# A third bank for the sums: the bias written ahead by ScalarE, and weight pieces that pass through the transposes' banks

## The chip, the cores and the metric

The kernel runs on one core of a Trainium2 chip. The metric is the device time of one execution in microseconds (us); of the kernel before there are three runs, 358.68, 358.79 and 359.64, so the median is 358.79. The engines are named as in the profile: PE (TensorE; PEld its weight loads), DVE (VectorE), ACT (ScalarE), POOL (GpSimd) and SP (SyncE, which only issues DMAs here).

## The reference

The input x has 8 images of 1024 rows and 512 columns in f32. Of attention only the first 16 rows of an image reach the output (the array `iter_out` is zero beyond row E = 16), so the work is nearly all in the second half, which is done for all rows:

```
mod = (silu(c) @ wmod)                          # per image: sa, ca, ga, sb, cb, gb
h = layernorm(x) * (1 + ca) + sa
x = x + ga' * attention(h)                      # beyond row 16: x + ga' * bo
h = layernorm(x) * (1 + cb) + sb
xd, wd = h and weight, each block of 32 rounded to a grid of 6 bits and scaled back
x = x + gb' * (xd @ wd.T + bias)                # ga', gb': sign(g) * max(|g|, 0.25)
```

## The kernel before

There are 64 tiles of 128 rows, 4 to a group (16 groups), 8 to an image. One loop over q = 0 to 63 is written out by hand on each engine; "slot q" is what an engine does in that turn of the loop. All waits are on semaphores, and every engine works strictly in the written order.

For tile n the work is this. ACT sums and squares the rows (`sums`, `deviations`), DVE makes the scale (`scales`, L1198 to L1201), ACT normalises (`normalise`, L501), POOL multiplies and adds the modulation (L390, L397), DVE takes the block maxima, quantises and scales back (L1208, L1227, L1234; half of the last on POOL, L377). PE turns the tile with four transposes (`transposes`, L730) into one of two PSUM banks, 0 and 1. ACT copies the turned tile rounded to XH (`high_part`, L469), DVE subtracts XH and writes the remainder XL (`low_part`, L1184). PE then sums in one of two PSUM banks, 2 and 3 (`product`): eight matmuls from XH (L747, L748), four from XL (L752), and a thirteenth, L755, that adds gate times bias from the small matrix G. DVE adds the sum to x (`add_tile`, L1241), and SP stores a group.

The weights are scaled by the gate for each image and split as well into WH and WL, in four pieces. Images are counted from 0. For images 2 to 7, and for the unscaled weights that the first 16 rows need (counted as 8), the turned weights lie in SBUF; a piece costs ACT two instructions, the rounded copy WH (L479) and a copy to PSUM bank 4 (L481), and DVE one, WL (L1193). The table FOLDS gives the slots: image b's pieces are issued in slots 8b-4 to 8b-1, image 8's in slots 57 to 60. "Fold slots" below are these.

PE's order in slot q is: transposes of tile q+1, the product of tile q, then a piece of the attention work for the first rows (`head_work`). ACT's is: `high_part(q+1)`, a weight piece, attention work, normalising, deviations, sums. DVE's is: `add_tile(q-1)`, `low_part(q+1)`, a weight piece, the small scales, maxima, quantising, attention work. The attention work has three passes in slots 9 to 53 and a last part in slots 52 to 61 (AFTER = 51). `masks_row` (L1020) is a copy of a 2x640 array with conversion, which the attention needs at slot 15.

## Time and profile before

| what | value |
|---|---|
| median of three runs | 358.79 us |
| the profiled execution's own time | 358.5 us |
| its span (first to last instruction) | 356.7 us |
| PE busy | 320.0 us (90%) |
| DVE busy | 284.8 us (80%) |
| ACT busy | 239.4 us (67%) |
| POOL busy | 240.6 us (67%) |
| L755, the bias matmul | 64 of them, 25.2 us, 393 ns each |
| chain that ended last | PE 38%, DVE 25%, ACT 16%, POOL 9%, issue 9% |

A matmul's duration in the profile is longer than the step from one to the next, since matmuls overlap; what a matmul costs on a busy PE is the step between two starts. Idle time is given before the instruction that ended it, with what released it. The granted clock (PEclk) is 1.00 in most of the span.

### The profile page before, as it was taken

Reading aid. Unit: us, or ns where it says so; the run is one execution under the profiler, and the core shown is the slowest. Engines: PE = TensorE matmul, PEld = TensorE weight load, DVE = VectorE, ACT = ScalarE, POOL = GpSimd, SP = SyncE. Lnnn points to the kernel's source line nnn. Section 1 sums busy time; section 2 is a strip of 40 time slices with the busy share of each in tenths; the row PEclk is TensorE's granted clock in tenths of the full one; section 3 lists DMA queues with packets and bytes.
Section 4 is the critical chain, followed back from the end, with each engine's and each line's share of the span. In section 5 each row is a group of like instructions: output and inputs, shape, how many; then the busy total and the mean of one; then the engine's idle time right before and its main releaser. Section 6 shows DMA issues by size and latency. Waiting matters only on the chain.

```text
span 356.7 us, 6296 instructions
## 1 busy us (share of the span) xinstructions
PE 320.0 (90%) x2247; PEld 243.4 (68%) x2247; DVE 284.8 (80%) x498; ACT 239.4 (67%) x537; POOL 240.6 (67%) x142
## 2 busy tenths in 40 slices
PE   7997984958999989998999999979999989994994
PEld 5223653748998777786788778767887768673883
DVE  4899839947727997969898879797878989899832
ACT  3357463577968798789788899876779897231410
POOL 2339956059876896989599979984999499702000
PEclk9999998798999999999999999989999999999899
DMA  6999899972697097958698977597837962020122
GB/s 207 395 405 367 277 214 234 314 237 112 120 218 197 2 239 204 222 152 217 183 242 265 242 136 291 154 233 158 257 120 152 233 180 115 6 86 31 73 105 88
DMA packets 23797, 68.51 MB, mean 192 GB/s; under 512 B 2467, under 2 KB 2596, under 8 KB 19798
## 3 DMA queue, kind: packets, MB, share of 16 engines
q1 hardware_dynamic: 16224, 53.40, 43.8%
q0 software_dynamic: 7392, 14.68, 24.9%
q8 instruction: 18, 0.29, 0.3%
q14 instruction: 13, 0.11, 0.1%
q10 hardware_dynamic: 150, 0.02, 0.0%
HBM read 50.96 MB, written 17.14 MB: 191 GB/s over the span
## 4 chain that ended last, share of the span: by engine, by line
PE 38%; DVE 25%; ACT 16%; POOL 9%; issue 9%; DMA 1%; SPq 0%; DVEq 0%; POOLq 0%; ACTq 0%
PE ps L747 7%; PE ps L748 7%; PE ps L752 7%; ACT U L501 5%; PE ps L730 4%; ACT unused L514 3%; DVE XL L1184 3%; PE ps L832 3%; POOL U L390 3%; DVE DD L1234 2%; DVE Q L1227 2%; DVE amax L1208 2%; ACT XH L469 2%; DVE X L1241 2%; POOL U L397 2%
## 5 line engine op out<-in xcount | busy, mean ns | idle before, releaser
L747 PE MATMUL ps<-WH,XH 128*128 128x512 f32 x256 | 108.4, 424 | 6.0 <-DVE X L1241 4.2
L748 PE MATMUL ps<-WL,XH 128*128 128x512 f32 x256 | 102.4, 400 | 0.0
L390 POOL TENSOR_TENSOR U<-U,c_bc 128x1024 f32<-128x1024 f32 x31 | 76.4, 2466 | 19.7 <-ACT U L501 19.6
L397 POOL TENSOR_TENSOR U<-U,sb_bc 128x1024 f32<-128x1024 f32 x31 | 74.2, 2394 | 4.5 <-POOL U L390 0.2
L1184 DVE TENSOR_TENSOR XL<-ps,XH 128x512 fp32r<-128x512 f32 x64 | 43.9, 685 | 40.4 <-ACT XH L469 40.3
L752 PE MATMUL ps<-WH,XL 128*128 128x512 f32 x256 | 69.4, 393 | 1.5 <-DVE XL L1184 1.5
L469 ACT ACTIVATE XH<-ps 128x512 fp32r<-128x512 f32 x64 | 37.5, 586 | 47.5 <-PE ps L730 47.3
L501 ACT ACTIVATE U<-X,nmr,rstd 128x512 f32<-128x512 f32 x64 | 48.2, 807 | 28.6 <-DVE nmr L1201 26.0
L747 PEld LDWEIGHTS ps<-WH,XH 128*128 128x128 f32 x256 | 49.7, 194 | 17.1 <-DVE X L1241 5.4
L752 PEld LDWEIGHTS ps<-WH,XL 128*128 128x128 f32 x256 | 48.6, 190 | 12.7 <-DVE XL L1184 1.9
L748 PEld LDWEIGHTS ps<-WL,XH 128*128 128x128 f32 x256 | 49.8, 195 | 8.8
L1241 DVE TENSOR_TENSOR X<-ps,X 128x512 f32<-128x512 f32 x64 | 43.6, 681 | 5.1 <-PE ps L755 4.9
L525 ACT ACTIVATE unused<-X,negm 128x512 bf16<-128x512 f32 x64 | 45.6, 714 | 0.5
L730 PE MATMUL ps<-idf,DD 128*128 128x128 f32 x256 | 40.7, 284 | 5.3 <-DVE DD L1234 5.3
L514 ACT ACTIVATE unused<-X 128x512 bf16<-128x512 f32 x64 | 39.5, 619 | 5.6 <-POOL X L354 5.1
L1208 DVE TENSOR_REDUCE amax<-U 128x32 f32<-128x1024 f32 x32 | 38.7, 1210 | 4.4 <-POOL U L397 4.4
L730 PEld LDWEIGHTS ps<-idf,DD 128*128 128x128 f32 x256 | 31.9, 147 | 13.2 <-issue 8.4
L1227 DVE TENSOR_TENSOR Q<-U,ps 128x1024 fp8e4<-128x1024 f32 x32 | 39.0, 1218 | 0.2
L377 POOL TENSOR_TENSOR DD<-Q,s 128x1024 f32<-128x1024 fp8e4 x12 | 23.0, 1913 | 19.9 <-DVE Q L1227 19.9
L413 POOL TENSOR_TENSOR Wd<-Wb,gb_bc 128x512 f32<-128x512 f32 x24 | 30.3, 1293 | 3.8 <-issue 3.8
L1193 DVE TENSOR_TENSOR WL<-ps,WH 128x512 fp32r<-128x512 f32 x36 | 24.4, 685 | 3.4 <-ACT ps L481 3.2
L755 PE MATMUL ps<-G,pick 128*128 128x512 f32 x64 | 25.2, 393 | 0.0
(232 smaller groups left out, 443.8 us busy)
## 6 DMA issues: line engine op xcount, KB each, us to landing
X<-in_x SPq DMA_DIRECT2D x16, 1024.0 KB, 7.5
out<-X SPq DMA_DIRECT2D x15, 1024.0 KB, 6.0
X<-mod_scratch POOLq DMA_DIRECT2D x14, 1024.0 KB, 13.6
X<-in_wmod SPq DMA_DIRECT2D x2, 1024.0 KB, 12.2
sb_bc<-mod_scratch SPq DMA_DIRECT2D x7, 256.0 KB, 12.9
c_bc<-mod_scratch SPq DMA_DIRECT2D x7, 256.0 KB, 11.2
gb_bc<-mod_scratch SPq DMA_DIRECT2D x6, 256.0 KB, 5.7
X<-in_wmod SPq DMA_DIRECT2D x2, 512.0 KB, 4.7
```

The source lines that it names most:

```text
L390: nc.gpsimd.tensor_tensor(a, a, spread(c_bc[:, b % 2, :]), ALU.mult).then_inc(u_done, 2 if g == 0 else 1)
L397: nc.gpsimd.tensor_tensor(a, a, spread(sb_bc[:, b % 2, :]), ALU.add).then_inc(h_done, 2 if g == 0 else 1)
L501: A.activation(U[:, g % 2, j, :], X1[:, g % XSLOTS, j, :], ACT.Identity, bias=nmr[:, g % 2, j:j + 1], scale=rstd[:, g % 2, j:j + 1]).then_ ...
L514: A.activation(unused[:, j % 2, :], X1[:, g % XSLOTS, j, :], ACT.Identity, accum_out=total[:, j:j + 1]).then_inc(sum_done, 1)
L730: m = TR(ps[:, XT_BANK + n % 2, c * P:(c + 1) * P], DD[:, j, c * P:(c + 1) * P], idf[:])
L747: M(bank, XH[:, n % 2, r], WH[:, b % 2, k, :], start=k == 0, stop=False)
L748: M(bank, XH[:, n % 2, r], WL[:, b % 2, k, :], start=False, stop=False)
L752: M(bank, XL[:, n % 2, r], WH[:, b % 2, k, :], start=False, stop=False)
L1184: TT(XL[:, n % 2, :], ps[:, XT_BANK + n % 2, :], XH[:, n % 2, :].bitcast(F32), ALU.subtract).then_inc(xl_done, 1)
L1208: RED(amax[:, h, :], blocks(U[:, g % 2, HALF * h:HALF * (h + 1), :]), AX, ALU.max, apply_absolute_value=True).then_inc(am_done, 1)
L1227: TT(blocks(Q8[:, h]), blocks(U[:, g % 2, HALF * h:HALF * (h + 1), :]), wide(inv[:, h, :]), ALU.mult, saturate=False).then_inc(q_done, 1)
L1241: TT(a, ps[:, Y_BANK + n % 2, :], a, ALU.add).then_inc(o_done, 1)
```

## The change

From tile 16 on (WIDE) a sum rotates over three banks, 4, 2 and 3. ACT writes gate times bias, already spread over the 128 partitions, into the bank (`preset_bias`, in slot q for tile q+1, behind `high_part(q+1)` and the weight piece), and the product only adds to it: L755 goes for 48 tiles. The product waits for `preset` in place of the add of tile n-2; `preset_bias(n)` waits for the add of tile n-3. Six more DMAs on SP (256 KB each) bring the spread rows, into `v_bc` and a new tensor. Bank 4 is no longer free for the weights: from image 2 on a piece goes through bank 0 or 1, the one that tile q's transposes left, and the transposes of tile n wait for WL of the piece whose slot in FOLDS is n-3. One matmul (`open_third`) opens bank 4. `masks` now lies in a part of U until the first tile needs it, so `masks_row` runs at the start, ahead of `bias_rows`. Some semaphores are merged.

```
+WIDE = 16
+        bias_odd = sb("bias_odd", [P, D])
+        bias_bc = (v_bc[:], bias_odd[:])
+        mk = U[0:2, 0, 2:4, :].rearrange("p j d -> p (j d)")[:, 0:P + D]
+        def sum_bank(n):
+            return Y_BANK + n % 2 if n < WIDE else (W_BANK, Y_BANK, Y_BANK + 1)[(n - WIDE) % 3]
+        def piece_bank(q):
+            return XT_BANK + q % 2
@@ SP, in the loop over t
                     mod_row(gb_bc[:], b, GB, gb_in)
+                    if b == 2:
+                        sp.wait_ge(x1_done, 3)
+                    if b >= 4:
+                        sp.wait_ge(preset, 2 * TILES * (b - 1) - WIDE)
+                    mod_row(bias_bc[b % 2], b, GBIAS, bias_in[b % 2])
@@ ACT, weight_high
-                    act.wait_ge(wt_low, NC * b + k)
+                    act.wait_ge(xl_done, fold_slot(b, k) + 2)
                     A.copy(ps[:, bank, :], turned(b, k)).then_inc(w_copied, 1)
+            def preset_bias(n):
+                b = n // (2 * TILES)
+                act.wait_ge(bias_in[b % 2], 16 * (b // 2))
+                if n == WIDE:
+                    act.wait_ge(wt_mm, 3 * NC + 1)
+                else:
+                    act.wait_ge(o_done, n - 2)
+                A.copy(ps[:, sum_bank(n), :], bias_bc[b % 2]).then_inc(preset, 1)
             def normalise(g, h):
+                if g == 0 and h == 1:
+                    act.wait_ge(lrow_done, 1)
@@ ACT, slot q
-                    weight_high(*FOLDS[q - 1], W_BANK)
+                    b, k = FOLDS[q - 1]
+                    weight_high(b, k, W_BANK if b == 1 else piece_bank(q))
+                if WIDE <= q + 1 < LAST:
+                    preset_bias(q + 1)
@@ PE, transposes(n)
                     pe.wait_ge(xl_done, n - 1)
+                    if n - 3 in FOLDS and FOLDS[n - 3][0] > 1:
+                        b, k = FOLDS[n - 3]
+                        pe.wait_ge(wt_low, NC * b + k + 1)
@@ PE, product(n)
+                opens = n < WIDE
+                if not opens:
+                    pe.wait_ge(preset, n - WIDE + 1)
+                elif n >= 2:
                     pe.wait_ge(o_done, n - 1)
...
-                M(bank, pick[:, b:b + 1].to_broadcast([P, P]), G[:], start=False, stop=True).then_inc(y_done, 1)
+                if opens:
+                    m = M(bank, pick[:, b:b + 1].to_broadcast([P, P]), G[:], start=False, stop=True)
+                m.then_inc(y_done, 1)
+            def open_third():
+                pe.wait_ge(plain_cp, NC)
+                M(ps[:, W_BANK, :], onesr[:], G[:], start=True, stop=True).then_inc(wt_mm, 1)
+                if q == WIDE - 3:
+                    open_third()
@@ DVE
-                elif q == 1:
-                    masks_row()
...
             first_v()
+            masks_row()
             bias_rows()
-                    weight_low(*FOLDS[q - 1], W_BANK)
+                    b, k = FOLDS[q - 1]
+                    weight_low(b, k, W_BANK if b == 1 else piece_bank(q))
```

How this stands in ACT's order in slot 20 (a fold slot of image 3), up to slot 21's first row. XH is the turned tile, WH and the copy from Wd the weight piece, U the normalising. Before:

```order
L469 ACTIVATE XH<-ps 128x512 [waits xt_done,y_done]
L479 ACTIVATE WH<-Wd 128x512 [waits wscaled,y_done]
L481 COPY ps<-Wd 128x512 [waits wt_low]
L501 ACTIVATE U<-X,nmr,rstd 128x512 x2
L514 ACTIVATE unused,total<-X 128x512 [waits sum_done,x_added2]
L514 ACTIVATE unused,total<-X 128x512 [waits sum_done]
L469 ACTIVATE XH<-ps 128x512 [waits xt_done,y_done]
```

And now:

```order
L488 ACTIVATE XH<-ps 128x512 [waits xt_done,y_done]
L498 ACTIVATE WH<-Wd 128x512 [waits wscaled,y_done]
L501 COPY ps<-Wd 128x512 [waits xl_done]
L514 COPY ps<-v_bc 128x512 [waits o_done,bias_in0]
L534 ACTIVATE U<-X,nmr,rstd 128x512 x2
L547 ACTIVATE unused,total<-X 128x512 [waits sum_done,x_added2]
L547 ACTIVATE unused,total<-X 128x512 [waits sum_done]
L488 ACTIVATE XH<-ps 128x512 [waits xt_done,y_done]
```

One copy of 128x512 has come in behind the piece, ahead of the normalising.

On PE, slot 21: tile 22's transposes, tile 21's product, and the next slot's transposes (DD is the tile, idf the identity). Before:

```order
L730 MATMUL ps<-idf,DD 128x128 [waits xd1_done,xl_done]
L730 MATMUL ps<-idf,DD 128x128 x3
L747 MATMUL ps<-WH,XH 128x512 [waits xh_done,o_done]
...
L755 MATMUL ps<-G,pick 128x512
L730 MATMUL ps<-idf,DD 128x128 [waits xd1_done,xl_done]
```

And now:

```order
L770 MATMUL ps<-idf,DD 128x128 [waits xd1_done,wt_low,xl_done]
L770 MATMUL ps<-idf,DD 128x128 x3
L790 MATMUL ps<-WH,XH 128x512 [waits xh_done,preset]
...
L796 MATMUL ps<-WH,XL 128x512 x3
L770 MATMUL ps<-idf,DD 128x128 [waits xd1_done,wt_low,xl_done]
```

L755 has gone, the product waits for the copy on ACT, and the transposes that stand ahead of the product wait for DVE's weight piece too.

On DVE near the start, X being the first half tile, LR the bias rows and Wd the weights. Before:

```order
L984 TENSOR_TENSOR X<-X,v_bc 128x1024 [waits x_in0,v_row]
L1000 CAST LR<-lrow 1x512 [waits rows_ok,cleared]
L1002 TENSOR_TENSOR LR<-lrow,LR 1x512 [waits lrow_done]
L1000 CAST LR<-lrow 1x512
L1002 TENSOR_TENSOR LR<-lrow,LR 1x512 [waits lrow_done]
L929 TENSOR_REDUCE ps<-Wd 128x32 [waits w_in]
```

And now:

```order
L1038 TENSOR_TENSOR X<-X,v_bc 128x1024 [waits x_in0,v_row]
L1074 CAST mkr<-U 2x640 [waits mk_in]
L1054 CAST LR<-lrow 1x512 [waits rows_ok,cleared]
L1056 TENSOR_TENSOR LR<-lrow,LR 1x512 [waits lrow_done]
L1054 CAST LR<-lrow 1x512
L1056 TENSOR_TENSOR LR<-lrow,LR 1x512 [waits lrow_done]
L983 TENSOR_REDUCE ps<-Wd 128x32 [waits w_in]
```

The conversion of the masks has come here from slot 1, where it stood between two tiles' work.

## Rows read from the trace of the kernel before

**Rows 1.** Busy time by stretch: stretch, length, engines with counts, clock, DMA

```profile
140.00:300.00 160.00, 153.49 (x1415) 122.72 (x1413) 137.41 (x234) 132.83 (x295) 138.51 (x73) 0.99 0.77 194
230.00:240.00 10.00, 7.93 (x35) 6.28 (x35) 9.93 (x15) 7.87 (x21) 8.63 (x4) 0.83 0.95 225
300.00:332.00 32.00, 26.55 (x121) 20.16 (x119) 29.96 (x49) 9.97 (x19) 11.24 (x6) 0.97 0.16 66
```

**Rows 2.** Waits of ACT from 135 to 294 us: total, times, longest

```profile
ACT U L501 <- DVE nmr L1201: 15.7, 9, 3.0
ACT XH L469 <- PE ps L730: 7.9, 8, 2.0
```

**Rows 3.** Timeline, slot 1 of DVE: start, us, engine, line, names, count, idle before

```profile
56.80 2.15 DVE L1020 CAST mkr<-mk 2x640 fp32r<-2x640 f32 x1
58.88 0.67 DVE L1241 TENSOR_TENSOR X<-ps,X 128x512 f32<-128x512 f32 x1
61.43 1.09 PE L730 MATMUL ps<-idf,DD 128*128 128x128 f32 x4 [5.31 <-DVE DD L1234]
```

**Rows 4.** Timeline at the start: DVE's first conversions and POOL beside them

```profile
12.91 3.39 POOL L354 TENSOR_TENSOR X<-X,v_bc 128x1024 f32<-128x1024 f32 x1 [10.43 <-DVE v_bc L980]
14.01 2.57 DVE L1000 CAST LR<-lrow 1x512 fp32r<-1x512 f32 x1
17.32 0.41 DVE L1000 CAST LR<-lrow 1x512 fp32r<-1x512 f32 x1
```

**Rows 5.** Timeline, slots 19 to 22

```profile
153.45 0.40 PE L747 MATMUL ps<-WH,XH 128*128 128x512 f32 x1
153.68 0.39 PE L748 MATMUL ps<-WL,XH 128*128 128x512 f32 x1
154.93 0.58 ACT L469 ACTIVATE XH<-ps 128x512 fp32r<-128x512 f32 x1
155.65 0.47 PE L747 MATMUL ps<-WH,XH 128*128 128x512 f32 x1
160.04 0.66 PE L730 MATMUL ps<-idf,DD 128*128 128x128 f32 x4
160.34 0.58 ACT L481 COPY ps<-Wd 128x512 f32<-128x512 f32 x1
160.86 1.52 ACT L501 ACTIVATE U<-X,nmr,rstd 128x512 f32<-128x512 f32 x2
161.05 0.69 DVE L1193 TENSOR_TENSOR WL<-ps,WH 128x512 fp32r<-128x512 f32 x1 [0.34 <-ACT ps L481]
168.79 0.66 PE L675 MATMUL ps<-idf,late 128*128 128x128 f32 x4 [1.07 <-DVE late L1105]
```

**Rows 6.** Waits of ACT from 154 to 222 us

```profile
ACT U L501 <- DVE nmr L1201: 5.2, 4, 2.4
ACT XH L469 <- PE ps L730: 2.8, 3, 1.5
```

**Rows 7.** Timeline, tile 35: its XH and its product's start

```profile
218.30 0.58 ACT L469 ACTIVATE XH<-ps 128x512 fp32r<-128x512 f32 x1
220.13 0.48 PE L747 MATMUL ps<-WH,XH 128*128 128x512 f32 x1
```

**Rows 8.** Timeline, slot 37 (image 5's first fold slots)

```profile
228.02 0.60 PE L730 MATMUL ps<-idf,DD 128*128 128x128 f32 x4
228.85 0.69 DVE L1193 TENSOR_TENSOR WL<-ps,WH 128x512 fp32r<-128x512 f32 x1 [0.35 <-ACT ps L481]
```

**Rows 9.** Timeline, slots 58 and 59

```profile
324.31 0.50 PE L747 MATMUL ps<-WH,XH 128*128 128x512 f32 x1 [2.08 <-DVE X L1241]
331.24 1.06 PE L730 MATMUL ps<-idf,DD 128*128 128x128 f32 x4
332.12 0.68 DVE L1193 TENSOR_TENSOR WL<-ps,WH 128x512 fp32r<-128x512 f32 x1
```

More of the change, by code:

```diff
@@ L173, in build @@
         sb_in = [sem(f"sb_in{i}") for i in range(2)]
+        bias_in = [sem(f"bias_in{i}") for i in range(2)]
         wmod_in = [sem(f"wmod_in{i}") for i in range(7)]
@@ L185, in build @@
         (ga_mm, cs_mm, rows_mm, rows_cp, gate_mm, v_row, cs_rows, gb_col, rows_turned, columns_cp,
-         columns_out, cs_out, g_rows, u_first, h_first, xd1_done, s32_done) = (
+         columns_out, cs_out, g_rows, first_h, xd1_done, s32_done) = (
             sem(n) for n in (
                 "ga_mm", "cs_mm", "rows_mm", "rows_cp", "gate_mm", "v_row", "cs_rows", "gb_col",
-                "rows_turned", "columns_cp", "columns_out", "cs_out", "g_rows", "u_first",
-                "h_first", "xd1_done", "s32_done"))
-        bd_done, hs_sa, bdm_done, w_grid, gb_in, plain_cp, w_copied = (
-            sem(n) for n in ("bd_done", "hs_sa", "bdm_done", "w_grid", "gb_in", "plain_cp", "w_copied"))
+                "rows_turned", "columns_cp", "columns_out", "cs_out", "g_rows", "first_h", "xd1_done", "s32_done"))
+        bd_done, hs_sa, bdm_done, w_grid, gb_in, preset, plain_cp, w_copied = (
+            sem(n) for n in ("bd_done", "hs_sa", "bdm_done", "w_grid", "gb_in", "preset", "plain_cp", "w_copied"))
         (exp_c, silu_done, mod_mm, wd_done, wscaled, wt_mm,
@@ L453, in _ @@
             act.dma_start(lrow[:], rows).then_inc(vec_in, 16)
-            act.dma_start(mk[:], masks).then_inc(mk_in, 16)
+            act.dma_start(mk, masks).then_inc(mk_in, 16)
             act.wait_ge(c_loaded, 16)
@@ L734, in product @@
                 b = n // (2 * TILES)
-                bank = ps[:, Y_BANK + n % 2, :]
+                bank = ps[:, sum_bank(n), :]
                 if n % (2 * TILES) == 0:
@@ L746, in product @@
                     r = slice(k * P, (k + 1) * P)
-                    M(bank, XH[:, n % 2, r], WH[:, b % 2, k, :], start=k == 0, stop=False)
-                    M(bank, XH[:, n % 2, r], WL[:, b % 2, k, :], start=False, stop=False)
+                    M(bank, XH[:, n % 2, r], WH[:, b % 2, k, :], start=opens and k == 0, stop=False,
+                      skip_group_check=not opens)
+                    M(bank, XH[:, n % 2, r], WL[:, b % 2, k, :], start=False, stop=False, skip_group_check=not opens)
                 pe.wait_ge(xl_done, n + 1)
@@ L751, in product @@
                     r = slice(k * P, (k + 1) * P)
-                    M(bank, XL[:, n % 2, r], WH[:, b % 2, k, :], start=False, stop=False)
+                    m = M(bank, XL[:, n % 2, r], WH[:, b % 2, k, :], start=False, stop=not opens and k == NC - 1,
+                          skip_group_check=not opens)
                 if n == 0:
                     pe.wait_ge(g_rows, 4)
-                M(bank, pick[:, b:b + 1].to_broadcast([P, P]), G[:], start=False, stop=True).then_inc(y_done, 1)
+                if opens:
[4 more added lines that the diff above has]
+                M(ps[:, W_BANK, :], onesr[:], G[:], start=True, stop=True).then_inc(wt_mm, 1)
             def project(bank, state, dg, row, signal):
@@ L1031, in first_modulate @@
                 dve.wait_ge(cs_mm, 1)
-                TT(a, spread(C_BANK), a, ALU.mult).then_inc(u_first, 1)
-                dve.wait_ge(u_first, 1)
+                TT(a, spread(C_BANK), a, ALU.mult).then_inc(first_h, 1)
+                dve.wait_ge(first_h, 1)
                 dve.wait_ge(cs_mm, 2)
-                TT(a, a, spread(S_BANK), ALU.add).then_inc(h_first, 1)
+                TT(a, a, spread(S_BANK), ALU.add).then_inc(first_h, 1)
             def spread(bank):
@@ L1087, in attend @@
                                  ex.rearrange("p q c t -> p (q c t)")).then_inc(eT_done, 1)
-                    RED(st[:, 6, 0:16], ex.rearrange("p q c t -> p (q c) t"), AX, ALU.add).then_inc(esum_done, 1)
-                    dve.wait_ge(esum_done, i + 1)
-                    REC(st[:, 7, 0:16], st[:, 6, 0:16]).then_inc(einv_done, 1)
+                    RED(st[:, 6, 0:16], ex.rearrange("p q c t -> p (q c) t"), AX, ALU.add).then_inc(e_step, 1)
+                    dve.wait_ge(e_step, 2 * i + 1)
+                    REC(st[:, 7, 0:16], st[:, 6, 0:16]).then_inc(e_step, 1)
                 elif o == 12:
-                    dve.wait_ge(einv_done, i + 1)
+                    dve.wait_ge(e_step, 2 * i + 2)
                     dve.wait_ge(pv_mm, i + 1)
@@ L1204, in maxima @@
                 if g == 0 and h == 0:
-                    dve.wait_ge(h_first, 1)
+                    dve.wait_ge(first_h, 2)
                 else:
@@ L1240, in add_tile @@
                 a = X1[:, g % XSLOTS, j, :]
-                TT(a, ps[:, Y_BANK + n % 2, :], a, ALU.add).then_inc(o_done, 1)
+                TT(a, ps[:, sum_bank(n), :], a, ALU.add).then_inc(o_done, 1)
             early_constants()
             first_v()
+            masks_row()
             bias_rows()
```

22 lines of the change are left out of this document (10 added, 12 removed).

## The prediction

> **What bounds the kernel now.** I read the busy time by stretch first, then the waits of each engine, then the timeline slot by slot. From 140 to 300 us PE is busy 153.5 of 160 us, DVE 137.4 and ACT 132.8 [rows 1]. PE is the fullest, but by little: a gain on PE alone soon meets the other two. From 300 to 332 us it is DVE, 30.0 of 32 us, while ACT has only 10.0 [rows 1]. ACT's 25 idle us or so in the long stretch are of two kinds [rows 2]: 7.9 us in which XH waits for the transposes, which is real slack, and 15.7 us in which normalising waits for the small scale that DVE computes behind its own XL. That second kind is a round trip between the engines, and only partly there to be filled.
>
> **The change part by part.** Durations are of the one profiled execution; its own time is 358.5 us, 0.3 below the median of the runs.
>
> *The bias matmul.* Between the starts of two matmuls of 512 columns lie 153.68 - 153.45 = 0.23 us [rows 5]. That, and not the duration of 0.39, is what one costs on a full PE. 48 of them are 11.0 us.
>
> *The copy on ACT.* The trace has the same shape, 128x512 from SBUF to PSUM: from the start of L481 to the next start is 160.86 - 160.34 = 0.52 us [rows 5]. 48 copies are 25 us, 8 in each image, on an engine with about 27 idle us in the stretch where 40 of them fall. If all are hidden they cost nothing. From below, a gain through the copy alone is excluded, since it is added work. From above it is 25 us.
>
> *Slots 20 to 35, where ACT binds.* XH of tile 20 ends at 155.51 and the product starts at 155.65: 0.14 of slack. Now that product also needs the copy behind XH. From there to 222 us ACT idles 2.8 us for transposes (all usable) and 5.2 us for DVE in four waits [rows 6]. In each of those four the copy hides once, 4 x 0.52 = 2.1; the rest of the wait is DVE's XL and its three small scales, which still follow XH. 15 copies are 7.8 us, less 2.8, less 2.1, so ACT comes 2.9 us later to tile 35. There it had 220.13 - 218.88 = 1.25 us of slack [rows 7], of which the copy takes 0.52 and 0.14 was there at the start, which gives back 0.6. The product of tile 35 starts 2.3 us later against that of tile 20, although PE itself would save 15 x 0.23 = 3.5. This is the place where the forecast is decided. With ACT's waits on DVE fully usable the term would be -0.8 or, PE setting the pace, down to -3.5; with none usable +4.4.
>
> *Weight pieces through the transposes' banks.* A new wait, on PE, ahead of the product: the transposes of tile n stand in order before the product of tile n-1, so while they wait for WL of the piece, that product stands too, and behind it everything on PE; ACT and DVE then wait for XH of tile n. Before, the product could start its eight XH matmuls (8 x 0.23 = 1.8 us) while DVE was still at XL; now XL and the piece behind it must both be done. In slot 21 the transposes began at 160.04 and WL ended at 161.05 + 0.69 = 161.74, 1.7 us later [rows 5]. In slot 37 it is 229.54 - 228.02 = 1.5 us [rows 8]. Within a group of four fold slots the first such stall delays PE and thereby gives the later ones their slack, so I count one per group: bounds 0 and 1.7 (where ACT is late by as much anyway, it costs nothing: in slots 20 to 35 it is contained in ACT's lateness). I take 1.0 for image 2's group, where PE waits a moment later for the attention work in any case, and 1.4 each for images 5 and 6.
>
> *Tiles 13 to 19.* +1.0 for the group, +0.2 for the opening matmul, then four products without L755, -0.9.
>
> *Tiles 36 to 52.* 17 x 0.23 = 3.9 saved, two groups 2.8: -1.1. ACT has fewer sums there, and should follow.
>
> *Tiles 53 to 58.* DVE is full [rows 1] and its work is the same: 0.
>
> *The end.* The third bank lets product 58 off its 2.08 us wait for the add [rows 9], which was the point of a third bank. But the transposes of tile 59, in front of it, now wait for WL. In slot 59 the transposes began at 331.24 and WL ended at 332.12 + 0.68 = 332.80: 1.5 us later [rows 9]. The last five products save 5 x 0.23 = 1.1. Sum +0.4.
>
> *The masks.* The conversion stood between two tiles and took 2.15 us, the next instruction starting 2.08 later, in front of the block for which PE waited 5.31 us [rows 3]. That goes: -2.1 in front of a PE that was waiting, and POOL's next half, done at about 58.6, does not come in between by more than 0.2. At its new place the question is what it costs. The first conversion there took 2.57 us and the second of the same shape 0.41; POOL's add ran from 12.91 to 16.30 [rows 4], and the first conversion ended just after. So a conversion waits for POOL's instruction to end, and the first in line pays. With the masks in front they pay, and the row conversions behind take 0.41 each: 640 columns against 512 make about 0.5 added. DVE runs without a gap there up to the first tile, so 0.5 reaches it. If instead each conversion cost its own 2.15, the move would return nothing (0 for the sum of both places).
>
> The Trainium skill says it as a rule ("SBUF — State Buffer", section "SBUF: two separate sides"): a VectorE instruction that uses both ports and a GpSimd instruction exclude each other for the whole instruction. By that rule the sum of the move is -1.6, by the bare duration of the row 0. The two conversions of one shape, 2.57 and 0.41, agree with it.
>
> *DMAs.* Six more loads of 256 KB on SP, behind loads of the same kind that have slots to spare; the wait of SP for `preset` comes where the SP program waits for later work anyway. 0; a late bias row would stop ACT, and I see none.
>
> *Sum.* -1.6 (masks) +1.2 (tiles 13 to 15) -0.9 (16 to 19) +2.3 (20 to 35) -1.1 (36 to 52) +0 +0.4 (end) = +0.3. 358.5 + 0.3 = 358.8 on the profile's own time, 359.1 against the median.
>
> **The rivals.** What a measurement of this kernel can tell from no change is about 0.3%, 1.1 us.
>
> A, *PE stays the bound.* ACT fits the copies into its idle time. For it: 7.9 + 15.7 us of waits against some 19 us of copies in that stretch [rows 2]. Against it: the waits on DVE are round trips. Then 48 x 0.23 = 11.0 less six tiles under DVE (1.4) = -9.6, masks -1.6, tiles 13 to 15 +1.2, a fold stall in slot 21 +1.7 and in images 5 and 6 +1.4 (the second half of these is taken up), end +1.5: 358.5 - 5.4 = 353.1 us.
>
> B, *ACT becomes the bound* and its waits for DVE do not shrink beyond the copy that hides in each. Place: slots 15 to 51. 37 x 0.52 = 19.2, less 7.9, less 9 x 0.52 = 4.7, gives +6.6; about 2.0 come back, as the XH copies were some 2.5 us ahead of the products at slot 51 and now need be ahead by one copy only. With masks -1.6, tiles 13 to 15 +1.2 and the end +0.4: 363.1 us, slower. It decides from the point where more than about 60% of the 15.7 us [rows 2] stay. For it: DVE, nearly as full, is the one waited for; and a late XH makes the next scale late too.
>
> C, *the clock.* From 230 to 240 us, after PE idled about 2 us, the granted clock was 0.83, that is, for part of the stretch at 1.2 instead of 2.4 GHz [rows 1], which cost up to 1.7 us. New stalls of 1.5 us stand in each fold group; six drops of 1.7 would make 10 and 369 us. Against it: PE waited 1.07 us at 168.79 [rows 5] in a stretch whose mean is 0.99, and the new stalls are shorter than the one that had one. The Trainium skill's page "TensorE: Matmul & The Clock Gate" ("A second HAM failure mode: psum-queue depth-cycling") describes a kernel in which small idles while PSUM banks rotate made the clock swing; by that rule this is the likely outcome, but the kernel already rotates two banks at a mean of 0.99 [rows 1].
>
> That the change does not do what it says I exclude but for the masks: L755 is gone from 48 products and one copy has come in for each. If the masks' move returns nothing, add 1.6 to the forecast.
>
> **Numbers.** Forecast (saving and new waits nearly cancel, 356.5 to 361.5): 0.46, of which 0.10 below 357.7, 0.24 within 0.3%, 0.12 above 359.9. A: 0.27, faster. B: 0.22, slower. C: 0.02, slower. The remaining 0.03 is a small difference that comes about otherwise, within 0.3%. So faster 0.37, same 0.27, slower 0.36. The time is that of the forecast, 359.1; the range reaches A's and B's values, 352.8 to 363.3, and the forecast's own range is 356.5 to 361.5.
>
> **What would show it.** Right: the masks' conversion ends within 0.6 us of where the row conversion ended, and tile 4's transposes start 1.3 to 1.9 us earlier. In slots 20 to 35 ACT has almost no idle time and products start right behind a copy. In fold slots the transposes wait for L1193's counterpart by 1 to 1.7 us. ACT is busy above 92% from 140 to 300 us, PE below 94%. Wrong, towards A: the steps between products without attention work are 3.2 us in most slots, and ACT's waits for the scale fall below 5 us. Wrong, towards B: they stay above 9 us and XH's waits for transposes vanish. C: the granted clock under 0.97 in the long stretch. What would upset the whole: a gain or a loss that arises before tile 13 and is not the masks'.

## The result, and the profile after

The changed kernel takes 366.78 us, the median of 4 runs (364.34 to 370.16); the kernel before took 359.22 us on the same chip (358.68 to 361.11). By the medians it is slower by 7.6 us. The ratio of 1.018, with an interval from 1.011 to 1.025, is that of the fast runs, which leaves out the slow one of 370.16, and it stands for 6.4 us. The change is slower clear of noise; whether by more or less than 2% is not settled. The forecast was 359.1 us, with a range from 352.8 to 363.3. The profiled execution is the fastest of the four, 364.3 us with a span of 362.5, so 5.8 us of span have to be found against the 356.7 of before.

The head of the page: the span, busy time of the engines, and the granted clock in 40 slices. Then the chain that ended last, by engine, and three groups of instructions.

```profile
span 362.5 us, 6304 instructions
PE 312.0 (86%) x2200; PEld 234.0 (65%) x2200; DVE 284.1 (78%) x498; ACT 263.8 (73%) x585; POOL 240.2 (66%) x142
...
PEclk9999998998999899999999999999899999996998
...
PE 29%; DVE 26%; ACT 24%; issue 11%; POOL 7%; DMA 1%; SPq 0%; DVEq 0%; ACTq 0%; POOLq 0%
...
L790 PE MATMUL ps<-WH,XH 128*128 128x512 f32 x256 | 109.7, 429 | 4.8 <-ACT ps L514 4.4
...
L1236 DVE TENSOR_TENSOR XL<-ps,XH 128x512 fp32r<-128x512 f32 x64 | 43.9, 686 | 46.0 <-ACT XH L488 45.9
...
L770 PE MATMUL ps<-idf,DD 128*128 128x128 f32 x256 | 39.9, 280 | 24.9 <-DVE XL L1236 13.2
```

PE does 8 us less work than before (320.0) and still ends later; on the chain its share falls from 38 to 29% and ACT's rises from 16 to 24%. The clock row has its dips as before, one or two slices long. The last row says where: ahead of the transposes (now L770) PE idles 24.9 us. The same group idled 5.3 us before, all of it once, ahead of tile 4 [rows 3]; that wait is 3.3 us now, and the other 21.6 us, in 14 waits, are new. Ahead of the products PE idles 4.8 us, 4.4 of them for the bias copy (L514).

The stretches, with the columns of [rows 1]:

```profile
140.00:300.00 160.00, 142.22 (x1360) 111.90 (x1360) 133.64 (x226) 147.85 (x325) 134.03 (x70) 0.99 0.80 200
...
250.00:260.00 10.00, 8.91 (x41) 7.09 (x40) 7.16 (x13) 9.25 (x23) 9.43 (x5) 0.83 0.95 258
300.00:332.00 32.00, 25.02 (x115) 18.34 (x114) 28.69 (x48) 15.24 (x28) 13.90 (x8) 0.96 0.16 67
```

In the long stretch ACT has become the fullest engine, 147.9 of 160 us (before 132.8), PE has fallen to 142.2 from 153.5 and DVE to 133.6 from 137.4 [rows 1]. The mean clock of the long stretch is 0.99 as before; its one slow place has moved from 230 to 250 us. ACT's waits from 138 to 302 us, against [rows 2]:

```profile
ACT U L534 <- DVE nmr L1253: 9.1, 9, 1.8
ACT XH L488 <- PE ps L770: 3.6, 6, 1.3
```

ACT still waits nine times for DVE's scale, but shorter, 9.1 us instead of 15.7.

Slots 20 and 21, the place of [rows 5] (timeline: start, duration, engine, line, idle before):

```profile
156.00 0.59 ACT L514 COPY ps<-v_bc 128x512 f32<-128x512 f32 x1
156.64 0.50 PE L790 MATMUL ps<-WH,XH 128*128 128x512 f32 x1 [1.39 <-ACT ps L514]
...
159.32 0.61 ACT L547 ACTIVATE unused<-X 128x512 bf16<-128x512 f32 x1
159.58 1.29 PE L870 MATMUL ps<-late,sq 32*32 32x32 f32 x128
...
159.93 0.57 ACT L488 ACTIVATE XH<-ps 128x512 fp32r<-128x512 f32 x1
160.41 0.62 ACT L498 ACTIVATE WH<-Wd 128x512 fp32r<-128x512 f32 x1
...
160.93 0.58 ACT L501 COPY ps<-Wd 128x512 f32<-128x512 f32 x1
161.44 0.58 ACT L514 COPY ps<-v_bc 128x512 f32<-128x512 f32 x1
161.64 0.69 DVE L1245 TENSOR_TENSOR WL<-ps,WH 128x512 fp32r<-128x512 f32 x1 [0.34 <-ACT ps L501]
...
162.43 0.63 PE L770 MATMUL ps<-idf,DD 128*128 128x128 f32 x4 [1.56 <-issue]
```

Read it backwards. The transposes start at 162.43, 0.10 after WL has ended (161.64 + 0.69 = 162.33). The profile writes "issue" or "DVE XL" as the releaser of such a wait, but by the times, and by the wait that the change adds, it is WL. WL waited for the piece's copy (L501). That stood on ACT behind WH and XH, and those behind the row sums (L547). So each fold slot is a ring over three engines: XH, WH and copy on ACT, XL and WL on DVE, then the transposes on PE. In the kernel before, the same transposes did not wait for WL and began 1.7 us before its end [rows 5].

A slot on PE is the transposes of the next tile and then the slot's own product. The worst case is the start of slot 58, where DVE is full:

```profile
330.13 0.68 DVE L1236 TENSOR_TENSOR XL<-ps,XH 128x512 fp32r<-128x512 f32 x1
330.73 0.68 DVE L1245 TENSOR_TENSOR WL<-ps,WH 128x512 fp32r<-128x512 f32 x1
331.32 1.21 DVE L1286 TENSOR_TENSOR DD<-Q,ps 128x1024 f32<-128x1024 fp8e4 x1
...
331.51 1.09 PE L770 MATMUL ps<-idf,DD 128*128 128x128 f32 x4 [5.22 <-DVE XL L1236]
```

DVE works without a gap up to WL, and PE stands for 5.22 us.

By the product's start, after minus before, the 5.8 us arise so. Each row counts from the start of the last product of the row above to the start of its own last product; the first counts from the start of the span, and the last ends with product 63:

| Tiles | Forecast | Measured |
|---|---|---|
| up to 12 (masks) | -1.6 | -1.6 |
| 13 to 15 | +1.2 | +2.1 |
| 16 to 19 | -0.9 | -0.7 |
| 20 to 35 | +2.3 | +2.4 |
| 36 to 52 | -1.1 | +2.2 |
| 53 to 58 | 0 | +3.5 |
| end | +0.4 | -2.1 |

The +2.4 of the fourth row looks like the forecast of +2.3, and it is not the same thing. The prediction spoke of the stretch from product 20 to product 35, and between those two starts the shift grows by 1.3 us (0.99 to 2.26). The other 1.1 is the step from product 19 to 20, the wait of 1.39 us for the first late bias copy, which is in the lines above.

### The profile page after: what moved, and what is told of

It reads as the page before. It is cut to its first block, busy times and chain, and to the rows that moved or that the text cites. A ratio compares the mean times of both kernels' runs of the same rounds, so it can differ in the third digit from the quotient of the medians.

```text
span 362.5 us, 6304 instructions
## 1 busy us (share of the span) xinstructions
PE 312.0 (86%) x2200; PEld 234.0 (65%) x2200; DVE 284.1 (78%) x498; ACT 263.8 (73%) x585; POOL 240.2 (66%) x142
## 4 chain that ended last, share of the span: by engine, by line
PE 29%; DVE 26%; ACT 24%; issue 11%; POOL 7%; DMA 1%; SPq 0%; DVEq 0%; ACTq 0%; POOLq 0%
ACT U L534 7%; PE ps L792 5%; PE ps L790 5%; PE ps L796 5%; ACT unused L547 5%; DVE XL L1236 4%; PE ps L770 3%; ACT XH L488 3%; PE ps L884 3%; DVE amax L1260 3%; ACT unused L558 3%; DVE Q L1279 2%; DVE DD L1286 2%; POOL U L409 2%; DVE X L1293 2%
## 5 line engine op out<-in xcount | busy, mean ns | idle before, releaser
L790 PE MATMUL ps<-WH,XH 128*128 128x512 f32 x256 | 109.7, 429 | 4.8 <-ACT ps L514 4.4
L792 PE MATMUL ps<-WL,XH 128*128 128x512 f32 x256 | 104.5, 408 | 0.0
L796 PE MATMUL ps<-WH,XL 128*128 128x512 f32 x256 | 70.6, 399 | 1.5 <-DVE XL L1236 1.5
L770 PE MATMUL ps<-idf,DD 128*128 128x128 f32 x256 | 39.9, 280 | 24.9 <-DVE XL L1236 13.2
L796 PEld LDWEIGHTS ps<-WH,XL 128*128 128x128 f32 x256 | 49.8, 195 | 13.4 <-DVE XL L1236 2.1
L770 PEld LDWEIGHTS ps<-idf,DD 128*128 128x128 f32 x256 | 29.5, 142 | 36.4 <-issue 17.2
L547 ACT ACTIVATE unused<-X 128x512 bf16<-128x512 f32 x64 | 39.5, 619 | 5.8 <-POOL X L373 5.1
L1286 DVE TENSOR_TENSOR DD<-Q,ps 128x1024 f32<-128x1024 fp8e4 x20 | 24.2, 1212 | 0.4
```

The lines of the kernel that those rows point to most:

```text
L547: A.activation(unused[:, j % 2, :], X1[:, g % XSLOTS, j, :], ACT.Identity, accum_out=total[:, j:j + 1]).then_inc(sum_done, 1)
L770: m = TR(ps[:, XT_BANK + n % 2, c * P:(c + 1) * P], DD[:, j, c * P:(c + 1) * P], idf[:])
L790: M(bank, XH[:, n % 2, r], WH[:, b % 2, k, :], start=opens and k == 0, stop=False, skip_group_check=not opens)
L792: M(bank, XH[:, n % 2, r], WL[:, b % 2, k, :], start=False, stop=False, skip_group_check=not opens)
L796: m = M(bank, XL[:, n % 2, r], WH[:, b % 2, k, :], start=False, stop=not opens and k == NC - 1, skip_group_check=not opens)
```

## The experiments

The kernel before had a median of 358.9 us beside the first four, and 358.9 to 359.2 beside the others. "Masks" below means the kernel that is the changed one with everything but the masks' move undone; most of the others add one part to it.

**Taking the change apart.** First the masks alone (e1), then on top of them one part each.

```diff
# e2_pieces: two sum banks, bias matmul kept, no bias copies
-            return Y_BANK + n % 2 if n < WIDE else (W_BANK, Y_BANK, Y_BANK + 1)[(n - WIDE) % 3]
+            return Y_BANK + n % 2
# e3_copy: bias copies, two sum banks, pieces in the weight bank
+                act.wait_ge(o_done, n - 1)
# e4_third: as e2, but with the three banks
```

> The changed kernel with everything undone but the early conversion of the masks (two sum banks, L755's counterpart in all 64 products, weight pieces through bank 4). By the changed kernel's trace the first 12 tiles gained 1.56 us; if nothing later eats it, 357.2 us against 358.8, ratio 0.9955. If the gain at tile 12 is lost in the waits between DVE and PE further on, ratio 1.000.

Measured 356.11 us (355.59 to 356.85), ratio 0.991 (0.989 to 0.994): 2.8 us faster than before, and 1.1 below the lower of the two times expected. The first transposes behind the masks' old place, which answer to those of [rows 3]:

```profile
58.38 1.21 DVE L1270 TENSOR_TENSOR DD<-Q,ps 128x1024 f32<-128x1024 fp8e4 x1
...
59.73 0.63 PE L758 MATMUL ps<-idf,DD 128*128 128x128 f32 x4 [3.24 <-DVE DD L1270]
```

They start 1.7 us earlier (61.43 before), and PE waits 3.24 instead of 5.31 us.

> e1 plus one thing: the weight pieces go through the transposes' banks, and the transposes wait for them. Theory W (this wait is the main loss): the fold groups lose 1.5 to 2 us each for seven groups, about +8 to +11 us against e1, so 366 to 368. Theory S (ScalarE's copies are the main loss): +2 to +3 us against e1, so 359 to 360.

Measured 362.95 us (362.43 to 363.72), ratio 1.011: 6.8 us over the masks. PE's longest waits:

```profile
PE ps L762 <- DVE XL L1224: 11.5, 6, 3.8
PE ps L762 <- issue: 5.8, 7, 1.7
PE ps L762 <- DVE DD L1274: 3.6, 2, 3.3
```

There are no bias copies in this kernel, and 17.3 of the changed kernel's 21.6 us of new waits are there already, in 13 waits (the last row is older: the masks' kernel has 3.6 us of it as well). The time lies between the two theories, 3 us short of W and 3 over S. The waits for the pieces are 6.8 of the 10.7 us between the masks' kernel and the changed one, so they are the main loss, as W said, but 17.3 us of waiting cost only 6.8 us of time.

> e1 plus one thing: the bias is copied ahead by ScalarE from tile 16 on and L755's counterpart goes, with two sum banks and bank 4 kept for the weights. Theory W: the copies hide in most of ScalarE's idle time and PE saves up to 11 us: -3 to -5 us against e1, 352 to 354. Theory S: ScalarE is late by its copies, +3 to +6 us against e1, 360 to 363.

Measured 370.43 us (367.31 to 373.33), ratio 1.029: 14.3 us over the masks, far outside both theories (352 to 354, 360 to 363). With two banks a bias copy must wait until DVE has emptied the bank, and everything behind it on ACT waits too:

```profile
PE ps L783 <- ACT ps L511: 20.0, 18, 3.1
```

The profiled execution is the slowest, 373.33 us, so these 20.0 are on the high side. The changed kernel, with a third bank, waits 4.4 us for its copies. Copies written in advance are thus only bearable with a third bank.

> The changed kernel without the copies on ScalarE: three sum banks, weight pieces through the transposes' banks, L755's counterpart in all 64 products. Against e2_pieces it has the third bank alone. Theory W: as e2 less 0 to 2 us (the adds that products waited for), 365 to 367. Theory S: 358 to 360. If the third bank is worth nothing while the transposes' wait stands in front of the product, it equals e2 within 0.5 us.

Measured 366.78 us (366.04 to 368.41), ratio 1.022: 3.8 us over e2, and the same as the changed kernel. The third bank by itself was expected to be worth 0 to 2 us. Nearly the whole difference arises in one slot (product 50 starts 0.6 us later than in e2, product 51 4.9):

```profile
293.80 0.87 PE L862 MATMUL ps<-late,sq 32*32 32x32 f32 x79 [0.36 <-DVE sq L1130]
298.13 0.90 PE L862 MATMUL ps<-late,sq 32*32 32x32 f32 x49 [3.46 <-issue]
```

PE stops inside a row of 128 independent small matmuls, after 79 of them, and nothing is waited for.

**Pieces without any bank.** If the pieces' low part is subtracted from the weights in SBUF, the copy of a piece, the shared bank and the wait all go.

```diff
# e5_direct (on the masks), e6_direct_all (on the changed kernel), e7_direct_third
-                    A.copy(ps[:, bank, :], turned(b, k)).then_inc(w_copied, 1)
...
-                TT(WL[:, b % 2, k, :], ps[:, bank, :], WH[:, b % 2, k, :].bitcast(F32),
+                TT(WL[:, b % 2, k, :], source, WH[:, b % 2, k, :].bitcast(F32),
```

> This is the kernel with only the masks moved (356.1 us), and in it the low part WL of the weight pieces of images 2 to 8 is subtracted by VectorE directly from the weights in SBUF. ScalarE's 28 copies into PSUM fall away, and no bank is shared. Theory W (of the pieces' change only the transposes' wait cost time; ScalarE's 28 copies of 0.52 us ran in spare time): 355 to 357 us. Theory S (ScalarE's work sets the pace of tiles 20 to 35, 16 copies of 0.52 us there): 348 to 351 us. Theory P (a subtraction with both operands in SBUF keeps GpSimd from its own SBUF reads, or is kept waiting by them): VectorE's WL shows over 0.9 us each instead of 0.69, the GpSimd groups of the folds get longer, and the time is 358 or more.

> The changed kernel (366.8 us) with its pieces' low part taken directly from SBUF in the same way: three sum banks and ScalarE's bias copies stay, the 28 copies of pieces and the transposes' wait go. Theory W: about the 6.8 us come back that the shared banks cost by themselves, 358 to 361 us, and PE has no idle time over 1 us ahead of the transposes in tiles 18 to 40. Theory S (ScalarE's bias copies are the larger part): the transposes' wait goes but product waits grow, 363 to 367.

> Three sum banks, no bias copies (the bias stays PE's last small matmul), pieces' low part directly from SBUF. Against the run with two banks and the direct pieces it holds the third bank alone. Theory W: the third bank does nothing, within 1 us of the two-bank run. Rival: the 3.5 us stop in slot 50 that the three-bank kernel with shared banks showed belongs to the third bank's program, and comes again: 3 to 4 us above the two-bank run.

Measured 370.0, 371.2 and 370.3 us, ratios 1.030, 1.035 and 1.032. Against the masks that is +13.9 us, by an edit that only takes work away from ScalarE. Theory P was right, and what was expected of e6 (358 to 367) failed with the others; e7 is within 1 us of e5, as expected. DVE's pieces in e5 (two groups, by where the weights lie), and one of them between GpSimd's instructions:

```profile
L1225 DVE TENSOR_TENSOR WL<-Wd,WH 128x512 fp32r<-128x512 f32 x24 | 35.3, 1471 | 0.0
L1225 DVE TENSOR_TENSOR WL<-Wb,WH 128x512 fp32r<-128x512 f32 x4 | 2.7, 682 | 0.0
```
```profile
166.17 2.40 POOL L403 TENSOR_TENSOR U<-U,c_bc 128x1024 f32<-128x1024 f32 x1
...
167.12 2.00 DVE L1225 TENSOR_TENSOR WL<-Wd,WH 128x512 fp32r<-128x512 f32 x1
168.71 2.64 POOL L410 TENSOR_TENSOR U<-U,sb_bc 128x1024 f32<-128x1024 f32 x1
```

The four pieces at the end, where GpSimd no longer works, take 0.68 us; the other 24 take 1.47 on average. The one shown should have ended at 167.80 and ended at 169.12, which is 0.55 after GpSimd's multiplication (166.17 + 2.40 = 168.57). It is so with every one: in 18 of the 24 a GpSimd multiplication or addition was running when WL began, and all 18 ended 0.55 to 0.57 us behind its end, however long it still ran; the six that met none took 0.67 or 0.68. GpSimd's next instruction, the addition, begun before WL had ended, takes 0.25 us more than the 2.39 that it took on average in the kernel before. So VectorE's instruction waits until GpSimd's is over. The Trainium skill says just this for a VectorE instruction with two SBUF inputs against a GpSimd instruction that reads SBUF ("SBUF — State Buffer", section "SBUF: two separate sides"); the trace agrees. The copy into PSUM, which looks superfluous, is what buys DVE its 0.69 us. In all three kernels DVE's extra 24 x 0.79 = 18.9 us cover up what the third bank and the bias copies do; the three times lie within 1.2 us of each other, and more than that they do not say.

**The piece ahead of the tile.** Does it help when the ring starts earlier?

```diff
# e8_early (on the changed kernel); the same swap on VectorE
+                piece = FOLDS.get(q - 1, (0, 0))
+                if piece[0] > 1:
+                    weight_high(*piece, piece_bank(q))
                 if q + 1 < LAST:
                     high_part(q + 1)
```

> The changed kernel in which ScalarE splits and copies a piece ahead of the high part XH of the next tile, and VectorE subtracts it ahead of XL. The piece is then split in a stretch in which both engines wait for the transposes anyway, and the transposes that wait for it find it done. Theory W: PE's 24.9 us ahead of the transposes shrink to 12 or less, 359 to 362 us. Rival (ScalarE's two instructions, 1.1 us, now delay XH by as much in each of the 28 slots): 366 to 372 us.

Measured 363.13 us (360.10 to 365.77), ratio 1.009 (1.006 to 1.013): 3.6 us better than the changed kernel by the medians, where 5 to 8 were expected, and the intervals of the two overlap. The same swap with the loads moved (e11 against e9, below) gives 1.7 us. The waits ahead of the transposes, in a profiled execution of 365.77 us:

```profile
PE ps L772 <- issue: 15.6, 11, 3.7
...
PE ps L872 <- issue: 3.7, 1, 3.7
PE ps L772 <- DVE DD L1288: 3.2, 1, 3.2
```

They fall from 24.9 to 18.8 us (the first and last row), not to 12. In slot 21 WL now runs from 160.63 to 161.32 instead of to 162.33, still waiting for ACT, whose row sums end only at 159.40. The order within the slot was worth a part; the pieces still come after ACT's long work.

**The stop in slot 50.** It came in e4 (3.46 us), in e8 (3.72), in e3 and e6 (2.25 and 1.95), and later in e14 (4.72). In e4 it comes after 79 of the 128 matmuls, in e6, e8 and e14 after 113, in e3 after 114. e4 keeps the bias matmul, 35 more in the tiles 16 to 50; e6, e8 and e14 have the one opening matmul of the third bank, e3 neither: 79 + 35 = 113 + 1 = 114. Counted from the start of the trace, exactly 1953 matmuls lie ahead of the stop in each of the five. So it stands at one fixed place of PE's instruction stream. What the DMA engines did, e4 from 290 to 298 us (queues: packets, MB, share of 16 engines), and the same stretch of e10:

```profile
q1 hardware_dynamic: 434, 1.46, 78.5%
q8 instruction: 1, 0.02, 0.8%
```
```profile
q8 instruction: 2, 0.03, 2.0%
```

The profile shows instructions as packets of 16 KB over the same DMA engines, and in e4 (as in e8) these were full until 295 us with 16 loads of the attention head's rows, issued in slots 44 to 49 for slot 55. The one such packet of e4's stretch, the 15th of its queue, began at 295.80, when the loads were nearly done, and PE went on at 298.13. In all five kernels the stop ends 2.3 to 2.5 us after this 15th packet began; in e10 it began at 291.94, ahead of the row. Moving these loads to slot 36 gives:

```diff
# e9_after_loads, e10_third_loads, e11_early_loads, e12_masks_loads
+                if t == 9:
                     for b in range(B):
                         for w0, w1 in ((GBIAS, V), (GB, ROWS)):
```

> The changed kernel with one edit: the 16 broadcast loads of msp rows (the attention head's modulation, needed in slot 55) are issued by SP at t = 9 (slots 36 to 40) instead of t = 11 (slots 44 to 49). Three kernels with three banks or bias copies stopped in the middle of slot 50's 128 small matmuls for 2 to 3.7 us with nothing waited for, while these loads held the DMA engines. Theory I (the engines' instructions come by the same DMA engines, and are late behind these loads): the changed kernel's median of 366.8, which lies 2.5 us over its own profiled run of 364.3 in which slot 50 did not stop, falls to 363 to 364.5. Rival (the stop has nothing to do with the loads): 366 to 368.

> The same move of the msp loads in the kernel with three banks and shared transposes' banks, without ScalarE's bias copies (366.8 us, of which 3.5 are the stop in slot 50 and some of the clock behind it). Theory I: no stop, 362.5 to 364. Rival: the stop stays, 366 to 368. Against the changed kernel with the same move it then gives what the bias copies and the 48 small matmuls that they replace are worth: theory W says within 1 us.

> The changed kernel with pieces split ahead of the high part (363.1 us, its profile has the stop in slot 50 of 3.7 us) and the msp loads moved. Theory I: 359 to 361. Rival: 362.5 to 364.

> The kernel with only the masks moved (356.1 us, no stop in slot 50) and the msp loads moved. Both theories: 355.5 to 356.7, since there was no stop; if the loads also held back other transfers it is below 355.5. It is the candidate for the fastest version.

Measured: e10 364.32 us (363.65 to 365.19) against e4's 366.78, ranges apart, and the row of small matmuls is whole:

```profile
294.59 1.29 PE L863 MATMUL ps<-late,sq 32*32 32x32 f32 x128 [0.37 <-DVE sq L1131]
```

Product 51 starts 4.3 us earlier against product 50's start than in e4. e9 is 365.54 (changed kernel 366.78; the intervals overlap), e11 363.89 (e8 363.13) and e12 357.32 (e1 356.11; 355.50 to 359.69 in 12 runs). Theory I's ranges were 362.5 to 364 for e10, 363 to 364.5 for e9, 359 to 361 for e11: none was met, e10's only by 0.3. So the move takes the stop out of e4, and brings no gain clear of noise in the others; e9's and e11's times do not bear theory I out. Of the 13 profiles with the loads at their old place five show the stop, all of kernels with a third bank or bias copies; of the four with the loads moved none does.

Two things follow from e9 and e10. The third bank alone, without the stop, is at 364.3 against e2's 363.0: no gain. By the product's starts e10 takes 218.75 us from product 15 to 63 and e2 218.79, so the 1.3 us are not the bank's. Bias copies instead of bias matmuls, 365.5 against 364.3, cost 1.2 us although PE has 47 matmuls less. The two ranges just touch, so this is at the edge of the noise; what is plain is that none of the 47 x 0.23 = 10.8 us came back.

**The last four pieces, and ScalarE's share.**

```diff
# e13_last_four (on e2)
-                    weight_high(b, k, W_BANK if b == 1 else piece_bank(q))
+                    weight_high(b, k, W_BANK if b in (1, B) else piece_bank(q))
# e14_after_light (on the changed kernel), e15_masks_light (on e1)
-                    A.activation(unused[:, j % 2, :], X1[:, g % XSLOTS, j, :], ACT.Identity,
+                    A.activation(unused[:, j % 2, 0:64], X1[:, g % XSLOTS, j, 0:64], ACT.Identity,
```

> The kernel with two sum banks and pieces through the transposes' banks (362.9 us), in which only the last four pieces (slots 56 to 59) go through the free weight bank again, with no transposes' wait there. Theory W: the waits of 3.76 and 1.91 us ahead of the transposes of slots 57 and 58 go. Slot 57 of the kernel with only the masks moved still has 2.0 and slot 58 1.4 us of another wait, so about 2.5 us come back: 360 to 361. What is then left over 356.1 (4 to 5 us) is the price of the six earlier groups. Rival (VectorE is full there, so the wait only changes its name): 362.5 to 363.5.

Measured 360.53 us (359.17 to 362.33), ratio 1.006: by the medians 2.4 us of the 6.8 are those of the last four pieces. Ahead of slot 58 the transposes no longer wait their 3.76 us; product 58 waits 2.06 us for its bank instead, and starts 2.0 us earlier against product 57, of which 0.4 is lost again behind it. The other 1.7 us between the two profiles arise ahead of product 15, where the program is the same, 1.0 of them because the clock fell there in e2 and not here. So the last four pieces cost 1.6 to 2.4 us, and the six earlier groups the rest.

> The changed kernel in which ScalarE's 64 row sums read 64 of 512 columns (7/8 of each mean's sum is left out), some 0.35 us less for each, 22 us of ScalarE's work in all. Theory S (ScalarE's queue sets the pace with the copies in it): 366.8 falls by 8 us or more, below 359. Theory W (VectorE's slot and PE's wait for it set the pace): it falls by 1 to 4 us, and the waits ahead of the transposes stay above 15 us.

> The kernel with only the masks moved (356.1 us) and the same lighter sums (7/8 of each sum left out). It says what ScalarE's time is worth without bias copies. Theory S: much less than in the changed kernel, 0 to 2 us. Theory W: about the same as there, 1 to 3 us.

Measured: the changed kernel falls by 10.4 us to 356.33 (352.94 to 360.26), the masks' kernel by 7.7 to 348.41 (348.35 to 348.69). The row sums of e14, and its waits (its profiled execution took 360.26 us, with the stop of 4.7 us in slot 50):

```profile
L547 ACT ACTIVATE unused<-X 128x64 bf16<-128x64 f32 x64 | 15.5, 244 | 7.5 <-POOL X L373 4.5 <-DMA X<-mod_scratch 3.0
```
```profile
PE ps L770 <- DVE XL L1236: 12.9, 6, 5.2
PE ps L770 <- issue: 5.3, 7, 1.5
```

39.5 - 15.5 = 24 us of ACT's work are worth 10.4 us with the bias copies and 7.7 us without. Both numbers are far above what theory W said, and 7.7 is also far above theory S's 0 to 2, so ACT sets the pace together with others in both kernels, a little more in the changed one: theory S is half right. In the masks' kernel the gain lies from product 35 to 52, 4.7 us, and from 20 to 35, 0.9; from 52 to 58 it is nothing (e15 against e12, in both of which the clock stayed high from product 12 to 58). But the waits ahead of the transposes, 18.2 us even so (with the 5.2 of slot 58 untouched), show that the shared banks cost their part on their own, and in slots with a full DVE all of it.

## Why the prediction was wrong

The account needs the time from one product's start to another's, in us, in five kernels. Each column adds one part to the one before it:

| Products | before | masks (e1) | + pieces (e2) | + third bank (e10) | + bias copies (changed) |
|---|---|---|---|---|---|
| 12 to 15 | 14.28 | 14.31 | 16.15 | 16.16 | 16.39 |
| 15 to 20 | 21.79 | 21.79 | 21.77 | 21.79 | 22.23 |
| 20 to 35 | 64.47 | 64.47 | 65.65 | 65.83 | 65.75 |
| 35 to 52 | 76.43 | 77.04 | 76.98 | 76.72 | 78.59 |
| 52 to 58 | 27.75 | 27.77 | 31.29 | 31.29 | 31.27 |
| 58 to 63 | 24.36 | 23.53 | 23.10 | 23.12 | 22.28 |

Where the clock does not differ and slot 50 does not stop, the rows of one program repeat within 0.3 us.

*The masks.* The mechanism was right: the conversion in front took 2.64 us, the next of 512 columns 0.41, where before the first of these took 2.57 [rows 4]: only the first in line pays. The size was too small. Alone (e1) the move gives 2.8 us, not 1.6. That the changed kernel shows -1.6 at tile 12 is luck: product 12 starts between 116.95 and 120.20 us in the 14 profiles with the masks moved and whole row sums, although their engines do the same up to there. What all of them show is the step from product 2 to 3, 5.7 to 7.2 us instead of 9.3.

*Tiles 13 to 15* cost 2.1 instead of 1.2. The stall of 2.52 us in slot 13 took the place of 2.0 us of other waits; behind it the clock fell, which it had not done there before:

```profile
120.00:132.00 12.00, 10.00 (x54) 8.05 (x53) 11.72 (x22) 11.37 (x27) 11.71 (x8) 1.00 0.65 159
```
```profile
120.00:132.00 12.00, 9.48 (x46) 7.61 (x45) 11.35 (x21) 9.47 (x25) 11.71 (x6) 0.86 0.76 176
```

e13 has the same stall without the fall, and takes 15.18 us for this row instead of e2's 16.15: the clock's part is 1.0 us.

*Slots 20 to 35* were to lose 2.3 us by the bias copies. They lost 1.3, and by the pieces: 1.2 in e2, nothing more with the copies, though PE had 15 matmuls less. The sign was that products start right behind a copy, and of the products 21 to 35 only the last does; the other copies ended 0.8 to 2.5 us before. ACT was nearly full, as forecast, but held PE up through XH and the pieces. In the long stretch 9.1 us of ACT's waits for DVE stayed, 58% of 15.7. That is B's sign (more than 9) by a hair; its other sign, that XH's waits vanish, did not come, 3.6 us are left.

*The first step that failed* is the term for tiles 36 to 52, -1.1, which measured +2.2. It took all 3.9 us of PE's saving, because "ACT has fewer sums there, and should follow". ACT did not follow. It is the engine that sets the pace there: lighter sums shorten this stretch by 4.7 us in the masks' kernel, against 0.9 in slots 20 to 35, and from product 35 to 49 by 4.2 in the changed one (65.00 to 60.82 in e14). With the copies the stretch takes 78.59 us against 76.72 without (e10), although PE has 17 matmuls less. The clock was low for 3.4 us in the one and not in the other. The kernel e9, where it was low for 10.2, takes 80.14; from the two I estimate 0.8 us for 3.4 us of low clock, so about 1 us is left for the copies, in place of a gain of 3.9. The two stalls of 1.4 us in this term were too dear: e2 and e10 are 0.3 to 0.6 us over e12 (76.41, the masks' kernel without a fall of the clock).

*The second step that failed* is "0" for tiles 53 to 58 because DVE's "work is the same" [rows 1]. It measured +3.5, and the table shows all of it as the price of the pieces. This term holds only as long as nobody waits for the last short thing in DVE's slot. The new wait made PE do so: image 7's group (slots 52 to 55), not priced at all, cost 1.6 us in e2, and ahead of product 58 PE stood 5.22 us where it had stood 2.08. What the third bank gives ahead of product 57 (0.8 us in e10) is lost again ahead of product 58, since the transposes' wait now stands in front of it.

*One stall per group* was also miscounted, though it is not what broke the sum. The sizes of two first stalls were right (1.56 us in slot 21, 2.24 in slot 37, forecast 1.7 and 1.5). But it was said that the first stall "gives the later ones their slack". In image 2's group there is a stall of 2.52 us, in image 3's of 1.56, 1.27 and 0.95, in image 4's of 1.26, in image 5's of 2.24, 1.46 and 0.68, in image 6's of 0.64 and 0.95, in image 7's of 1.18 and 0.48, in the last of 5.22 and 1.21. A likely reason is that the stall delays the transposes, hence XH on ACT, hence copy and WL, so that all three engines slip together and no slack arises. That chain is read from the timeline of slot 21 alone. And a stall's length is not its price: 4.5 us of them in images 5 and 6 of e2 cost 0.6 us at most, presumably because ACT would have been late by nearly as much.

*The end* was put at +0.4. Its sum leaves product 58's 2.08 us [rows 9] out without a word, as if the transposes' wait just took its place; that wait became 5.22. Behind product 58 the stall was 1.21 us (forecast 1.5) and five matmuls went (1.1), and a wait of 2.78 us for the attention work was absorbed. These make -2.7, and 2.1 us came back; the difference was not traced.

*The rivals.* A is excluded: PE's freed time brought nothing where three engines were within 10% of one another (133.6 to 147.9 us of 160). B's 363.1 us was closer than the forecast; ACT does set the pace from product 35 to 52, but most of the loss is the pieces' wait (6.8 us in e2), which B did not have. The clock (C) had some part. In the long stretch it cost one place, as before, not six. Over the whole span it was at the level of 1.2 GHz for 22.6 us against 17.0 before: newly behind the stall of slot 13 and in the last 2 us, and 6.8 us instead of 3.4 around slot 58.

What stays open: why the changed kernel's own runs spread from 364.3 to 370.2. The stop in slot 50 is absent from its profile, yet present, 4.72 us, in that of e14 with the same PE program; that some of its runs have it would explain part of the spread, but was not seen. Another part may lie at the start: the first product begins anywhere from 37.7 to 41.5 us in the profiles of kernels that do the same up to there.

The fastest version is e1, the masks' move alone: 356.1 us, 2.8 below the kernel before.

## What to carry to other kernels

Ask of each stretch which engine sets its pace before you price a wait or a saving in it. The same new wait cost 0.6 us at most where ScalarE was late anyway (tiles 36 to 52) and 3.5 us where VectorE was full (53 to 58); and matmuls taken from PE paid nothing where ScalarE paced the tiles. A lighter copy of the kernel, with part of one engine's work left out, shows the pace-setter better than busy shares do: 24 us of ScalarE's sums were worth 8 to 10 us, though it was busy only 68 to 73% of the span. Before handing a bank, a buffer or a port from one use to another, ask in which order its last user stands in its engine's program, and follow the new wait through every slot where it stands, the slots with "the same work" too. And take a stretch as shown only when two profiles of the same program agree on it: a single number at one tile can agree with a forecast by luck.

## What the runs showed of the hardware

- A VectorE subtraction of 128x512 with both operands in SBUF took 0.68 us beside an idle GpSimd. Where a GpSimd multiplication or addition was running when it began, it ended 0.55 to 0.57 us after that one, in 18 of 18 cases, and took up to 2.9 us (e5). With one operand in PSUM it took 0.68 or 0.69 in either case.
- PE ran dry for 2 to 4.7 us in a row of 128 matmuls of 32x32, behind exactly 1953 matmuls in each of five profiles, and went on 2.3 to 2.5 us after an instruction packet of 16 KB had begun behind a crowd of small loads on the DMA engines. The Trainium skill ("Runtime: NRT & Kernel Launch", section "Instruction fetch mechanics") describes the instruction store as filled in blocks of 16 KiB over a DMA queue of the engine's own, mostly hidden. The packets of 16 KB agree; that it stays hidden did not hold here, where the 128 matmuls and their weight loads are used up in 1.29 us.
- After PE had stopped for 3.46 us in e4 the granted clock was 0.50 for the next 2 us, the lower of its levels of 1.2 and 2.4 GHz (last column but two):

```profile
296.00:298.00 2.00, 0.00 (x0) 0.00 (x0) 1.46 (x2) 0.00 (x0) 2.00 (x3) 0.98 0.09 33
298.00:300.00 2.00, 1.87 (x54) 1.81 (x55) 0.00 (x0) 0.00 (x0) 2.00 (x2) 0.50 0.03 8
```
